# The gates' bias as a one-row product on TensorE, and maxima read from PSUM

## The reference

```python
gate_scores = x @ Wg + bg                    # 8 experts
_, idx = jax.lax.top_k(gate_scores, 2)
mask = jax.nn.one_hot(idx, E).sum(axis=-2)
h = gelu(einsum('td,edh->teh', xf, W1) + b1)
y = einsum('teh,ehd->ted', h, W2) + b2
out = einsum('ted,te->td', y, mask)          # sum of the two experts chosen
```

## Time and profile before

| | |
|---|---|
| median of 3 runs | 757.75 us |
| profiled execution, its span | 773.1 us |
| TensorE busy | 699.8 us, 91% |
| VectorE busy | 624.5 us, 81% |
| GpSimd busy | 584.0 us, 76% |
| ScalarE busy | 496.4 us, 64% |
| blocks 3 to 13 of the loop | 116.4 to 471.6 us, 32.3 us each |
| blocks 14 and 15 | 471.6 to 543 us |
| expert stage | 543 us to the end |

### The profile page before, as it was taken

How to read it: one execution, slowest core, us unless ns; L and a number is a source line. 1 busy time by engine, 2 the same in 40 slices (tenths; PEclk the granted TensorE clock), 3 DMA queues, 4 the chain that set the end, 5 groups by cost and what they waited for, 6 DMA issues and landing times. The chain is left out here.

```text
span 773.1 us, 17066 instructions
## 1 busy us (share of the span) xinstructions
PE 699.8 (91%) x5416; PEld 365.5 (47%) x5416; DVE 624.5 (81%) x1455; ACT 496.4 (64%) x898; POOL 584.0 (76%) x689
## 2 busy tenths in 40 slices
PE   4898999999999999999999999787979789999994
PEld 2222323333333333333333333231668679999994
DVE  4699899999999999999999999999677445545552
ACT  4656567777677775777767776544775346666663
POOL 7579495989879898798987988969476555667664
PEclk9999999999999999999999999997989789999998
DMA  7620000001010010100100001041322223333330
GB/s 272 212 65 28 12 18 14 28 29 56 15 43 28 29 56 15 43 28 29 56 15 29 29 15 43 15 138 42 88 68 75 81 81 94 88 86 98 100 90 1
DMA packets 47958, 45.42 MB, mean 59 GB/s; under 512 B 6981, under 2 KB 42576, under 8 KB 47872
## 3 DMA queue, kind: packets, MB, share of 16 engines
q1 hardware_dynamic: 41888, 31.60, 14.2%
q0 software_dynamic: 5984, 12.74, 4.5%
HBM read 27.73 MB, written 18.34 MB: 60 GB/s over the span
## 5 line engine op out<-in xcount | busy, mean ns | idle before, releaser
L744 ACT ACTIVATE e<-e 128x2048 f32<-128x2048 f32 x128 | 244.5, 1910 | 139.5 <-DVE e L946 132.6
L946 DVE SCALAR_TENSOR_TENSOR e<-scores_ps,bound_mem 128x2048 f32<-128x2048 f32 x128 | 292.2, 2283 | 25.6 <-PE scores_ps L436 23.8
L829 ACT ACTIVATE e<-scores_ps,bound_mem 128x128 f32<-128x128 f32 x364 | 104.4, 374 | 59.9 <-PE scores_ps L604 51.9
L1417 POOL DMA_INDIRECT out<-e,near x91 | 91.3, 1003 | 65.5 <-POOL near L1410 28.3
L455 PE MATMUL z_ps<-e,one_column 128*32 128x512 f32 x1024 | 136.0, 603 | 0.0
L1390 POOL TENSOR_TENSOR ctx_part<-ctx_part,z_inv 128x1024 f32<-128x1024 f32 x60 | 115.0, 1917 | 23.3 <-DVE z_inv L962 22.7
L1402 POOL TENSOR_TENSOR ctx_sum<-ctx_sum,ctx_part 128x512 f32<-128x512 f32 x90 | 115.8, 1287 | 6.0
L604 PE MATMUL scores_ps<-e,bound_mem 128*128 128x128 f32 x728 | 101.9, 284 | 8.7 <-ACT e L829 3.5
L604 PEld LDWEIGHTS scores_ps<-e,bound_mem 128*128 128x128 f32 x728 | 92.4, 198 | 12.0 <-issue 7.2
L954 DVE STREAM_TRANSPOSE ctx_part<-ctx_ps 128x512 f32<-128x512 f32 x128 | 90.3, 705 | 1.4 <-PE ctx_ps L448 1.3
L1364 POOL DMA_INDIRECT sorted_rows<-x_rows,slot x64 | 63.6, 994 | 27.2 <-issue 17.7
(11 more groups left out here) (171 smaller groups left out, 1032.1 us busy)
## 6 DMA issues: line engine op xcount, KB each, us to landing
near<-sorted_rows SPq DMA_DIRECT2D x91, 130.0 KB
near<-in_x SPq DMA_DIRECT2D x16, 256.0 KB, 2.7
bound_mem<-in_adjT SPq DMA_DIRECT2D x4, 1024.0 KB, 9.1
x_post<-in_x SPq DMA_DIRECT2D x16, 256.0 KB, 2.7
sorted_rows<-pad_row SPq DMA_DIRECT2D x1, 3640.0 KB, 14.7
out<-e,near POOLq DMA_INDIRECT x91
sorted_rows<-x_rows,slot POOLq DMA_INDIRECT x64
bound_mem<-in_w SPq DMA_DIRECT2D x1, 1024.0 KB
```

What stands on the lines that cost most here:

```text
L744: nc.scalar.activation(every, every, ACT.Exp, scale=SCORE_SCALE).then_inc(exp_done, 1)
L829: nc.scalar.activation(e_flat[:, h_at:h_at + P], scores_ps[:, i % 2, k * P:(k + 1) * P], ACT.Gelu, bias=part_flat[:, bias_at:bias_at + 1]) ...
L946: dve.scalar_tensor_tensor(out=e[:, s % E_RING], in0=scores_ps[:], scalar=-CLIP, in1=to, op0=ALU.max, op1=ALU.min).then_inc(clipped, 1)
L1417: nc.gpsimd.indirect_dma_start(out=out_rows, out_offset=bass.IndirectOffsetOnAxis(ap=near_u[:, id_at:id_at + 1], axis=0), in_=e_flat[:, at ...
```

## The change

TensorE adds the bias: ahead of each tile's gate product stands a product of `one_row` (1 x 128, all ones) with the bias row (1 x 35), which starts the sum in PSUM, and the gate product is added to it. VectorE's addition and its buffer `gates` go, with the semaphore between the addition and the maxima; the maxima and the positions read the gates from PSUM.

```diff
-        gates = sb("gates", [P, TILES, SPAN])
...
-        gate_filled, gate_drained = sem("gate_filled"), sem("gate_drained")
+        gate_filled = sem("gate_filled")
...
                 for t in range(TILES):
-                    ins = pe.matmul(job_ps[0][:, t * SPAN:(t + 1) * SPAN], xn2T[:, t * P:(t + 1) * P], wg_sb[:],
-                                    start=True, stop=True)
+                    to = job_ps[0][:, t * SPAN:(t + 1) * SPAN]
+                    pe.matmul(to, one_row[:], bg_row[0:1, 0, :], start=True, stop=False)
+                    ins = pe.matmul(to, xn2T[:, t * P:(t + 1) * P], wg_sb[:], start=False, stop=True)
                 ins.then_inc(gate_filled, 1)
...
-                dve.tensor_tensor(gates[:], job_ps[0][:, 0:TILES * SPAN].rearrange("p (t e) -> p t e", e=SPAN),
-                                  bg_row[:].to_broadcast([P, TILES, SPAN]), ALU.add).then_inc(gate_drained, 1)
-                dve.wait_ge(gate_drained, v + 1)
+                gates = job_ps[0][:, 0:TILES * SPAN].rearrange("p (t e) -> p t e", e=SPAN)
                 for t in range(TILES):
                     ins = dve.max(best[:, t, :], gates[:, t, :])
```

## The result

The changed kernel takes 791.14 us (median of 6 runs, 785.12 to 793.86) against 758.0 us for the kernel before (6 runs beside them, 757.08 to 761.39): a ratio of 1.0421 (95% interval 1.0393 to 1.045), 33 us slower. The forecast was 775.6 us, 762 to 786: the direction held, the time lies 15.5 us above the forecast and 5 us above the range.

The account below looks back on a forecast made before the run. VectorE was taken to end last by little around the change, with TensorE having 0.45 us slack. Loop 12.7 plus experts 5.1 gave 17.8 us: 773.1 became 790.9 profiled, 775.6 us at the median; range 762 to 786.

Parts of the forecast that it names:

- The price of the gate: On TensorE, the added bias products make each gate 1.7 us longer, 2.7 us after 1.01, at 0.45 us a tile.
- rival 1: In the gates, loads are laid under running products: 0.89 us added a gate, 763 us in all; chance 0.12.
- VectorE's gain: Each choose gets 0.26 us shorter: 0.30 us less for the addition, 0.04 us more for reading PSUM.
- Rival 4: In choose, PSUM reads cost 34 ns more each: 3 us in 13 chooses, 779 us in all; chance 0.06.
- The block: In the attention loop, blocks 3 to 13 each become 0.99 us longer, 10.9 us together.
- rival 3: TensorE's clock falls during the gate, 2.7 us more at half speed: 787 us (one block in three), 808 in all; chance 0.09.
- The expert stage: Gates 13 to 15 each cost 1.7 us more with nothing given back: 5.1 us, between 2 and 7.5.
- Blocks 14 and 15: At the loop's end, block 14 becomes 1.4 us longer and block 15 0.4 us longer.
- Carrying the difference to the median: Profiled execution is 15.35 us above the median of 757.75; that difference was carried over unscaled, 790.9 becoming 775.6 us.

Follow-up runs that it names:

- the first experiment: Changed kernel with the four one-row bias products side by side ahead of the four gate products: 768.37 us, 1.0135 to the kernel before.
- third experiments: Changed kernel with a 128-row stationary operand for the bias (first row ones, others zero), same order: 761.29 us, 1.0053 to the kernel before.
- The fourth experiment: Changed kernel with the loop's gate cut in two, two tiles at j = 1 and two at j = 2: 778.88 us, 1.0273 to the kernel before.
- experts alone: Kernel before with the change only in the last three blocks' gates, in the expert stage: 768.34 us, 1.0139 to the kernel before.
- changed kernel again: The changed kernel run once more with no edit: 791.04 us, 1.0449 to the kernel before.
- the loop alone: Kernel before with the change only in blocks 0 to 12, whose gates are in the attention loop: 784.23 us, 1.0346 to the kernel before.

## Why the prediction failed, point by point

- **The price of the gate: right.** 2.7 us forecast, 2.71 measured. The reading behind it, a change of the number of rows that leaves a load open in both directions, agrees with the first and third experiments: 0.115 us a change (0.69 / 6) or 0.10 (0.81 / 8), where 0.45 us a tile stands for 0.22 us and two changes of 0.115; and 0.22 us a pair when the rows don't change. That a load is left open is the explanation that fits, not something a row shows by itself. For rival 1 (loads laid under) the Trainium skill was named (TensorE: Matmul & The Clock Gate, Part 3, the mechanism); the 0.34 us a pair speak against loads pulled ahead across a change of rows.
- **VectorE's gain: right.** 0.26 us was forecast. By the means it is 0.31 (0.30 for the addition, 4 x 7 ns less for the maxima, 4 x 5 ns more for the positions), and the 4.55 us from clip to clip in place of 4.77 show 0.22. Rival 4, dear PSUM reads, falls, and with it the estimate of 65 ns a read worked out from the Trainium skill (VectorE: DVE Perf Modes, the TRN2 errata): 177 ns from PSUM, 184 from SBUF. The 34 ns of rival 4 were not the price of PSUM even before: beside the transposes of 705 and 671 ns the same view of the kernel before has those of `z_ps` (L959), from PSUM in the same shape, at 674.
- **The block: right where the clock holds.** 0.99 us a block was forecast; 33.26 in block 4 is 0.97 above the mean of before.
- **The failed step: rival 3.** "The clock falls" had a chance of 0.09 and stood outside the sum, because "In the loop it kept 2.4 GHz through gates of 1.0 us". That row says nothing of a run of 2.7 us, so for the long gate the sum held the clock at 2.4 GHz without a row behind it. Eight of eleven blocks had a fall, of 1.5 us each with one double: 379.53 - 11 x 33.28 = 13.4 us, 33.28 being the mean of undisturbed blocks. Rival 3 was mis-sized too: it took the gate itself to run at half speed, 2.7 us; in the loop the gate runs at 2.4 GHz (but for its last pair in three blocks) and the products behind it pay, scores 0.95 us and context 0.69 more in block 5. With its own condition, one block in three, it gave 787; by frequency and price as measured it is 8 of 11 and 1.5 us. The fourth experiment shows the cause: with the run cut in two, no falls. Why the same gate is followed by a fall in some blocks and not in others stays open.
- **The expert stage: too low, by the clock again.** 5.1 us forecast, with 7.5 as the top. Timed alone it costs 10.3. By profile, the time from the last clip is 224.5, 224.6, 220.5 and 220.6 us with the new form (changed kernel, experts alone, halves, changed kernel again), and 213.7 and 212.3 with the old one: 7 to 12 us. In the first 110 us of it the clock is 0.91, 0.91, 0.95 and 0.95 with the new form, 0.97 and 0.98 with the old: 20, 20, 11 and 11 us at 1.2 GHz, and 7 and 4. At 0.4 us each, the price that the two profiles of the changed kernel give, and this is an estimate, the four new forms would take some 216 us without that time and the two old ones some 211: 5 to 6 us for three longer gates, as forecast. The rest, 2 to 7 us, goes with the clock; gate 14 of the first profile is a part of it (4.4 us for 2.6), in the repetition only its first pair is slow. What brought the clock down in this stage, where TensorE also waits, was not tested.
- **Blocks 14 and 15: within 0.7 us.** Block 14, without a fall in this profile, lost 1.03 us (33.19 to 34.22; 1.4 forecast); block 15, from its first to its last clip, gained 0.3 (37.12 to 36.81; 0.4 lost forecast). In two other profiles of the long gate block 14 had a fall as well (35.83 us in the repetition, 35.58 with the loop alone).
- **Carrying the difference to the median: right, though the profiles seem to speak for the forecast.** The profiled spans differ by 18.7 us (791.8 - 773.1), nearly the 17.8 forecast, by accident: the profile of before carried 17 to 19 us too much in the experts, 10.2 of them in the three waits. The medians differ by 33: 13.4 of falls in the loop, 10.9 of added work there (24.3 in all), 1.0 and -0.3 for blocks 14 and 15, which leaves 8 for the experts, inside their 7 to 12 (the loop's figures are of an execution 2.7 us above that median).

## What to carry to other kernels

A small product that changes the number of stationary rows is paid at each change, so put such products together or make them one: here one product of 140 columns turned 33 us lost into 3 us won. When an edit lengthens a run of short products on TensorE, count the granted clock of what stands behind that run as a term of the sum and not as a remote rival, unless a row shows a run as long that kept the clock. And hold the span of a profile against the timed runs stage by stage before you compare two profiles: one of these carried some 18 us in its last stage, and its span was 13 us above the longest timed one.

## What the hardware showed that was not expected

- The clock fell with TensorE busy and not waiting: in block 5 of the changed kernel it was busy 34.59 of 34.77 us and had no idle time ahead of the scores that took 2.09 us. The Trainium skill (TensorE: Matmul & The Clock Gate, Why this matters for your kernels) names idle gaps between matmul bursts as what costs the clock; in these blocks the profile shows none (it models the ends of products, so short gaps inside the gate could be hidden in it). What preceded the falls was a run of loads, each followed by 35 columns. Blocks with a fall, of 11, by the length of that run: none for 1.0 us (before), 1.44 (one product), 1.90 (full rows) and two halves of 1.35 and 1.26; one for 2.02; eight, seven and nine for 2.71 (three profiles); five for 2.80 without uncovered loads.
- A fall can also come where no gate is: with full rows and with the loop alone block 1 had one (34.70 and 34.69 us), behind waits of 1.1, 0.8 and 2.2 us for VectorE. The kernel before waits as long at the same place, and its block 1 took 33.27 us without a fall.
- A stationary operand of one row costs no less than one of 128: 0.34 us a pair for both in the changed kernel, and 1.01 us for eight passes of either kind in the first experiment. With 128 rows throughout a pair is 0.22 us.
